# Tail of a two-stage image kernel: last tile normalised and split in three column pieces, output sum made by accumulating transposes

## The chip, the cores and the metric

The kernel runs on one core of a Trainium2 chip. The metric is the device time of one execution in microseconds (us), as the median of several runs. The core's engines run their own instruction streams and meet only at semaphores: TensorE (PE, with its weight loads shown apart as PEld), VectorE (DVE), ScalarE (ACT), GpSimd (POOL) and SyncE (SP), which here only issues DMAs.

## The reference, cut to what matters

The input `x` is (8, 32, 32, 64) float32. Two residual blocks follow each other:

```
x = x + diffusion(_gn(x), ...)     # 5 steps, then relu(bn(h))
x = x + conv(_gn(x), W, b)         # 3x3, 64 -> 64, ternary weights, relu(y + b)
return x
```

`_gn` subtracts the mean and divides by the standard deviation of each image and group of two channels. The second block is what the change touches: with x1 the output of the first block, it needs the statistics of x1, the normalised x1 (xn), the convolution of xn, `relu(alpha * conv + b)`, and at last x1 + that relu.

## The kernel before, in words

The eight images are two tiles of four (t = 0 and 1). The diffusion steps of the two tiles alternate in the order of the table `ORDER`; the last is step 4 of tile 1, so everything of the second block for tile 1 comes after all else. That tail is what the change is about.

Layout of the tail: a partition is one of a pair of image columns times a channel (2 x 64 = 128), the free dimension runs over 16 column pairs j, 32 rows h and 4 images b, so that one pair j takes 128 elements. Per tile:

- `residual` (DVE) adds x and the relu of block one into `coef[:, t, 2]` = x1 and takes its statistics; `spread` and `second_norm` (DVE with two small matmuls on PE and two tiny ACT operations) make scale and bias per image, and raise `norm_ready`.
- `normalise` writes xn into `odd_pairs(t)` = 17 shifted column pairs. The write crosses the two halves of the partitions: ACT does three operations of 64 x 512 and DVE five (its own four and the one for image 3), every one with a stride of four elements, since one operation takes one image. ACT counts `xn_ready`, DVE `xn_too`.
- `upper_half` (ACT) rounds xn to `hi`, `lower_half` (DVE) writes `lo` = xn - hi, in two pieces of columns each. For t = 1 the first piece has 5 of the 17 column pairs, the second 12.
- `dense(t, i)` (PE, line 1124) is the convolution: 12 matmuls of 512 columns per PSUM bank. Tile 0 has two parts of two banks (24 matmuls each), tile 1 has four parts of one bank (12 each), named `cf_t_i`.
- `relu_dense` (ACT) reads the PSUM of `cf_t_i` into `coef[:, t, 0]`. `output_sum` (DVE, line 851) adds x1 to it into `coef[:, t, 3]` and raises `sum_ready`. `out_natural(t, i)` (PE, line 957) transposes that back, 8 transposes for a part of tile 0 and 4 for one of tile 1, into `tb_t_i`; `take_out` (ACT) copies it to `coef[:, t, 4]`, and SP stores it (line 278).

PSUM has four slots. `job_table` gives each PE job its slot, and `take(name)` on PE waits until the reader of the job that held the slot before is done. `cf_0_1` and `cf_1_1` both have slot 3, `tb_0_0` and `cf_1_2` slot 0, `tb_0_1` and `cf_1_3` slot 1, `cf_0_0` and `cf_1_0` slot 2.

The order on each engine is written out by hand. In the tail it is:

```
ACT: normalise(1) upper_half(1) relu_dense(0,1) take_out(0,0) relu_dense(1,0) relu_dense(1,1) ...
DVE: normalise(1) output_sum(0,0) lower_half(1,0) lower_half(1,1) output_sum(0,1) output_sum(1,0..3)
PE:  dense(0,1) out_natural(0,0) dense(1,0) dense(1,1) out_natural(0,1) dense(1,2) out_natural(1,0)
     dense(1,3) out_natural(1,1) out_natural(1,2) out_natural(1,3)
```

All ACT operations go through one helper, so all have line 325.

Of the kernel before, what the change touches and what calls it, by code (L numbers as in the profile page):

```python
# [16 lines left out]
BT = B // TILES  # L17
# [61 lines left out]
def network(nc, x, wide_taps, norms, matrices, out_cols, conv_w, out):  # L79
# [11 lines left out]
    with ExitStack() as ctx:  # L91
# [3 lines left out]
        def sem(name):  # L95
            return ctx.enter_context(nc.semaphore(name))
# [71 lines left out]
        def part(ap, t, i):  # L168
            n = N // out_parts[t]
            return ap[:, i * n:(i + 1) * n]  # L170
# [5 lines left out]
        def odd_pairs(t):  # L176

            return coef[:, t, 3:5, :].rearrange("p a n -> p (a n)")[:, 0:(PAIRS + 1) * BT * H]

        def by_rows(ap, t, i):  # L180

            first = PAIRS // out_parts[t] + 1
            return ap.rearrange("p (j r) -> p j r", j=PAIRS + 1)[:, slice(0, first) if i == 0 else slice(first, None)]

        def slot_ap(name):
            return psum[:, slot_of[name], :]
# [28 lines left out]
            "wabs_ready", "kept_ready", "alpha_ready", "tern_ready"))  # L215
        mv_ready, q_ready, norm_ready, xn_ready, xh_ready, xl_ready = (sem(n) for n in (
            "mv_ready", "q_ready", "norm_ready", "xn_ready", "xh_ready", "xl_ready"))
        pads_ready, sum_ready = sem("pads_ready"), sem("sum_ready")

        edges_ready, xn_too = sem("edges_ready"), sem("xn_too")  # L220

        def wait_job(eng, name):

            eng.wait_ge(pe_job, job_no[name] + 1)

        def wait_reader(eng, name):

            eng.wait_ge(slot_free[slot_of[name]], uses_before[name] + 1)
# [86 lines left out]
        def _(act):  # L315
# [8 lines left out]
            def copy(dst, src, func=ACT.Copy, **kw):  # L324
                return nc.scalar.activation(dst, src, func, **kw)  # L325
# [144 lines left out]
                frees(copy(half(coef[:, t, 0, :], h), slot_ap(name), ACT.Relu, scale=outw[:, 2:3],  # L470
                           bias=outw[:, 3:4]), name)

            def normalise(t):

                act.wait_ge(norm_ready, t + 1)
                x1 = coef[:, t, 2, :].rearrange("p (j h b) -> p j h b", b=BT, h=H)
                to = odd_pairs(t).rearrange("p (j h b) -> p j h b", b=BT, h=H)
                for b in range(BT - 1):
                    copy(to[0:64, 1:, :, b], x1[64:128, :, :, b], ACT.Identity, scale=gn2[64:128, t, 3, b:b + 1],
                         bias=gn2[64:128, t, 4, b:b + 1]).then_inc(xn_ready, 1)  # L480

            def upper_half(t):

                act.wait_ge(pads_ready, 4)
                act.wait_ge(edges_ready, 2 * (t + 1))
                act.wait_ge(xn_ready, (BT - 1) * (t + 1))
                act.wait_ge(xn_too, (BT + 1) * (t + 1))
                for h in range(2):
                    if t:
                        wait_job(act, f"cf_0_{h}")  # L490
                    copy(by_rows(hi[:, :], t, h)[:, :, BT:BT + 128], by_rows(odd_pairs(t), t, h)).then_inc(xh_ready, 1)

            def relu_dense(t, h):

# [36 lines left out]
                wait_reader(act, f"nat_{k}_{t}_1")  # L531
                wrap(t, k + 1, halo_ready)
            rsqrt_first(128, BT)
            normalise(0)
            upper_half(0)
            relu_bn_out(1, 0)
            relu_bn_out(1, 1)
            relu_dense(0, 0)
            rsqrt_first(128, BT)
            normalise(1)  # L540
            upper_half(1)
            relu_dense(0, 1)
            take_out(0, 0)
            relu_dense(1, 0)
# [9 lines left out]
        def _(dve):  # L554
# [261 lines left out]
            def spread(t):  # L816

                wait_job(dve, f"mean2_{t}")
                frees(V.tensor_copy(gn2[:, t, 0, :], slot_ap(f"mean2_{t}")[:, 0:BT]), f"mean2_{t}")
                wait_reader(dve, f"mean2_{t}")  # L820
                then(V.tensor_tensor(gn2[:, t, 1, :], mv[:, t, :, 0], gn2[:, t, 0, :], ALU.subtract))
                then(V.tensor_tensor(gn2[:, t, 1, :], gn2[:, t, 1, :], gn2[:, t, 1, :], ALU.mult))
                signal(V.tensor_tensor(gn2[:, t, 2, :], mv[:, t, :, 1], gn2[:, t, 1, :], ALU.add), q_ready, t + 1)

            def second_norm(t):

                wait_job(dve, f"var2_{t}")
                rsqrt(128, BT, gn2[:, t, 3, :],
                      V.tensor_scalar(rs_in[:, 0:BT], slot_ap(f"var2_{t}")[:, 0:BT], GN2_EPS, None, ALU.add))
                leave(f"var2_{t}")  # L830
                signal(stt(gn2[:, t, 4, :], gn2[:, t, 0, :], -1.0, gn2[:, t, 3, :], ALU.mult, ALU.mult),
                       norm_ready, t + 1)

            def normalise(t):

                x1 = coef[:, t, 2, :].rearrange("p (j h b) -> p j h b", b=BT, h=H)
                to = odd_pairs(t).rearrange("p (j h b) -> p j h b", b=BT, h=H)
                for k, b in [(0, b) for b in range(BT)] + [(1, BT - 1)]:
                    p = slice(64 * k, 64 * k + 64)
                    V.tensor_scalar(to[64 * (1 - k):64 * (1 - k) + 64, k:k + PAIRS, :, b], x1[p, :, :, b],  # L840
                                    gn2[p, t, 3, b:b + 1], gn2[p, t, 4, b:b + 1], ALU.mult, ALU.add)\
                        .then_inc(xn_too, 1)

            def lower_half(t, h):
                dve.wait_ge(xh_ready, 2 * t + h + 1)
                V.tensor_tensor(by_rows(lo[:, :], t, h)[:, :, BT:BT + 128], by_rows(odd_pairs(t), t, h),  # L846
                                by_rows(hi[:, :], t, h)[:, :, BT:BT + 128].bitcast(f32), ALU.subtract).then_inc(xl_ready, 1)

            def output_sum(t, h):
                wait_reader(dve, f"cf_{t}_{h}")  # L850
                V.tensor_tensor(part(coef[:, t, 3, :], t, h), part(coef[:, t, 0, :], t, h),  # L851
                                part(coef[:, t, 2, :], t, h), ALU.add).then_inc(sum_ready, 1)

            def step(k, t, then_do=()):

                def then(i):
                    for at, what in then_do:
                        if at == i:
                            what()

                if k > 1 and not kept(k, t):
                    multiply(t, k + 1, A0, 0, 0)
                then(-1)
                if k == 0:
                    dve.wait_ge(s_halo, 4 * (t + 1))
                else:
                    dve.wait_ge(halo_ready, 4 * states_through(k - 1, t))
                for i, (a, dw, dc) in enumerate(((AYM, 0, -1), (AYP, 0, 1), (AXM, -1, 0), (AXP, 1, 0), (AE, 0, 0))):
                    multiply(t, k, a, dw, dc)
                    then(i)  # L870
                if k and k + 1 < STEPS and kept(k + 1, t):
                    dve.wait_ge(kept_free[t], k)
                    V.tensor_tensor(wc(first_two[t][:, :]), wc(coef[:, t, A0, :]), h_at(t, k), ALU.mult)\  # L873
                        .then_inc(kept_made[t], 1)
# [48 lines left out]
            for k, t in ORDER[2:-1]:  # L923
                step(k, t)
            residual(0)
            step(STEPS - 1, 1, ((-1, lambda: spread(0)), (1, lambda: second_norm(0)), (3, lambda: normalise(0))))
            lower_half(0, 0)
            lower_half(0, 1)
            residual(1)
            spread(1)  # L930
            second_norm(1)
            normalise(1)
            output_sum(0, 0)
            lower_half(1, 0)
            lower_half(1, 1)
            output_sum(0, 1)
            for q in range(4):
                output_sum(1, q)

        @blk.tensor  # L940
        def _(pe):
# [168 lines left out]
            def dense(t, i, first=0, last=None):  # L1110


                banks = 4 // out_parts[t]
                pe.wait_ge(xl_ready, 2 * t + 1 + (i > 0))
                dst = take(f"cf_{t}_{i}") if first == 0 else slot_ap(f"cf_{t}_{i}")
                for bank in range(banks):
                    j0 = 4 * (banks * i + bank)
                    to = dst[:, bank * BANK:(bank + 1) * BANK].rearrange("p (j r) -> p j r", r=128)
                    steps = [(b, dy, half_of) for b in range(2) for dy in range(3) for half_of in (hi, lo)]
                    for n, (b, dy, half_of) in enumerate(steps):  # L1120
                        if not first <= bank * len(steps) + n < (last or 1000):
                            continue
                        rows = half_of[:, :].rearrange("p (j r) -> p j r", j=PAIRS + 1)
                        ins = mm(to, dense_m[:, b, dy, :], rows[:, j0 + b:j0 + b + 4, dy * BT:dy * BT + 128],  # L1124
                                 start=(n == 0), stop=(n == len(steps) - 1))
                if last is None:
                    ins.then_inc(pe_job, 1)

            def out_natural(t, i):
                pe.wait_ge(sum_ready, out_parts[0] * t + i + 1)  # L1130
                src = part(coef[:, t, 3, :], t, i)
                turns(f"tb_{t}_{i}", [src[:, j * 128:j * 128 + 128] for j in range(16 // out_parts[t])])

            pe.wait_ge(mats_in, 16)
            def group_mean(t):
# [139 lines left out]
```

## Time and profile before

| | us |
|---|---|
| median of 3 runs | 340.66 (340.45, 340.66, 341.94) |
| the profiled execution, its own time | 342.05 |
| its span | 340.2 |
| PE busy / DVE busy / ACT busy | 258.7 / 270.1 / 137.3 |
| mean granted TensorE clock | 0.93 of full speed |

The span is the part of the execution that the trace covers; 342.05 - 340.2 = 1.85 us lie around it. A granted clock of 1.00 is 2.4 GHz and 0.50 is 1.2 GHz; TensorE has these two levels.

### The profile page before, as it was taken

Reading aid. Unit: us, or ns where it says so; the run is one execution under the profiler, and the core shown is the slowest. Engines: PE = TensorE matmul, PEld = TensorE weight load, DVE = VectorE, ACT = ScalarE, POOL = GpSimd, SP = SyncE. Lnnn points to the kernel's source line nnn. Section 1 sums busy time; section 2 is a strip of 40 time slices with the busy share of each in tenths; the row PEclk is TensorE's granted clock in tenths of the full one; section 3 lists DMA queues with packets and bytes.
Section 4 is the critical chain, followed back from the end, with each engine's and each line's share of the span. In section 5 each row is a group of like instructions: output and inputs, shape, how many; then the busy total and the mean of one; then the engine's idle time right before and its main releaser. Section 6 shows DMA issues by size and latency. Waiting matters only on the chain. (4 is left out here: it accounts for less than half of the span.)

```text
span 340.2 us, 4036 instructions
## 1 busy us (share of the span) xinstructions
PE 258.7 (76%) x1676; PEld 228.2 (67%) x1676; DVE 270.1 (79%) x224; ACT 137.3 (40%) x198; POOL 7.3 (2%) x25
## 2 busy tenths in 40 slices
PE   0116799929829799999502999999999987768794
PEld 0115688828728689668402999998989977656683
DVE  1895268848992575949999999999999999997811
ACT  3256579986002616260200332441522241452843
POOL 1000000000000000000100000110110000000000
PEclk9999899987958799999955899999999999999899
DMA  7596000000000000000230000633754003000033
GB/s 257 145 420 283 0 2 1 1 0 2 0 0 0 2 0 0 2 0 2 44 79 0 0 2 2 123 64 62 178 115 82 3 0 125 0 0 0 2 123 123
DMA packets 5169, 19.09 MB, mean 56 GB/s; under 512 B 2336, under 2 KB 2336, under 8 KB 3616
## 3 DMA queue, kind: packets, MB, share of 16 engines
q1 hardware_dynamic: 4144, 12.88, 10.6%
q0 software_dynamic: 720, 5.24, 7.6%
q10 hardware_dynamic: 288, 0.72, 0.7%
q8 instruction: 13, 0.21, 0.3%
q14 instruction: 4, 0.03, 0.0%
HBM read 11.50 MB, written 2.10 MB: 40 GB/s over the span
## 5 line engine op out<-in xcount | busy, mean ns | idle before, releaser
L797 DVE TENSOR_TENSOR ring<-coef,state 128x2048 f32<-128x2048 f32 x51 | 113.5, 2288 | 11.7 <-PE psum L1051 6.4
L1051 PE MATMUL psum<-mats,ring 128*128 128x128 f32 x816 | 94.5, 274 | 8.5 <-DVE ring L797 8.1
L1051 PEld LDWEIGHTS psum<-mats,ring 128*128 128x128 f32 x816 | 89.1, 141 | 12.3 <-DVE ring L797 12.0
L325 ACT ACTIVATE state<-psum 128x1024 f32<-128x1024 f32 x36 | 35.2, 1024 | 96.1 <-PE psum L1051 59.4
L1011 PE MATMUL psum<-coef,state 128*128 128x256 f32 x192 | 45.7, 390 | 0.0
L1011 PEld LDWEIGHTS psum<-coef,state 128*128 128x128 f32 x192 | 37.7, 196 | 5.4
L577 DVE SCALAR_TENSOR_TENSOR coef<-coef 128x2048 f32<-128x2048 f32 x15 | 34.4, 2291 | 3.4 <-ACT coef L325 3.1
L325 ACT ACTIVATE coef<-psum 128x512 f32<-128x512 f32 (+1 forms) x22 | 17.1, 789 | 39.7 <-PE psum L986 29.7
L1051 PE MATMUL psum<-mats,first_two 128*128 128x128 f32 x144 | 19.0, 290 | 18.6 <-DVE first_two L577 18.6
L986 PE MATMUL psum<-hi_s,sobel_m 128*128 128x512 f32 (+2 forms) x48 | 21.2, 446 | 13.2 <-DVE wred L581 7.4
L1051 PEld LDWEIGHTS psum<-mats,first_two 128*128 128x128 f32 x144 | 17.5, 151 | 19.1 <-issue 19.0
L986 PEld LDWEIGHTS psum<-hi_s,sobel_m 128*128 128x128 f32 x48 | 11.3, 236 | 16.1 <-issue 14.1
L1124 PE MATMUL psum<-hi,dense_m 128*128 128x512 f32 x48 | 20.4, 424 | 0.5 <-DVE lo L846 0.5
L1124 PE MATMUL psum<-lo,dense_m 128*128 128x512 f32 x48 | 19.8, 413 | 0.0
L986 PE MATMUL psum<-lo_s,sobel_m 128*128 128x512 f32 (+2 forms) x48 | 19.6, 430 | 0.0
L325 ACT ACTIVATE coef<-coef 128x2048 f32<-128x2048 f32 (+1 forms) x8 | 13.8, 1754 | 9.6 <-DVE coef L717 9.5
L325 ACT ACTIVATE coef<-coef,scales 128x384 f32<-128x384 f32 x32 | 16.7, 603 | 0.6 <-DMA coef<-in_wide_taps 0.6
L957 PE MATMUL psum<-mats,state 128*128 128x128 f32 x128 | 16.1, 282 | 0.3 <-ACT state L325 0.3
L957 PEld LDWEIGHTS psum<-mats,state 128*128 128x128 f32 x128 | 15.1, 147 | 0.6 <-ACT state L325 0.5
L325 ACT ACTIVATE ring<-state 128x2048 f32<-128x2048 f32 x4 | 11.4, 2854 | 5.9 <-DVE state L619 5.9
L851 DVE TENSOR_TENSOR coef<-coef 128x512 f32<-128x512 f32 (+1 forms) x6 | 5.2, 870 | 9.9 <-ACT coef L325 9.9
L986 PEld LDWEIGHTS psum<-lo_s,sobel_m 128*128 128x128 f32 x48 | 11.3, 235 | 2.0
(123 smaller groups left out, 273.9 us busy)
## 6 DMA issues: line engine op xcount, KB each, us to landing
coef<-in_wide_taps SPq DMA_DIRECT2D x4, 1536.0 KB, 11.5
first_two<-coef POOLq DMA_DIRECT2D x5, 1024.0 KB, 7.0
coef<-in_x SPq DMA_DIRECT2D x2, 1024.0 KB, 5.9
ring<-in_x SPq DMA_DIRECT2D x2, 512.0 KB, 7.0
ring<-in_x SPq DMA_DIRECT2D x1, 1024.0 KB, 9.6
out<-coef SPq DMA_DIRECT2D x2, 512.0 KB, 3.1
out<-coef SPq DMA_DIRECT2D x4, 256.0 KB, 3.0
mats<-in_matrices ACTq DMA_DIRECT2D x1, 384.0 KB, 6.6
```

What stands on the lines that cost most here:

```text
L325: return nc.scalar.activation(dst, src, func, **kw)
L577: return V.scalar_tensor_tensor(out=out_ap, in0=in0, scalar=scalar, in1=in1, op0=op0, op1=op1)
L797: V.tensor_tensor(wc(ring[:, slot, :]), wc(coef[:, t, a, :]), h_at(t, k, dw, dc), ALU.mult)\
L851: V.tensor_tensor(part(coef[:, t, 3, :], t, h), part(coef[:, t, 0, :], t, h), part(coef[:, t, 2, :], t, h), ALU.add).then_inc(sum_ready, 1)
L957: ins = nc.tensor.transpose(dst[:, j * 128:j * 128 + 128], src, ident)
L986: ins = mm(dst[:, bank * BANK + to * C:bank * BANK + (to + count) * C], sobel_m[:, m, :], part[:, frm * C:(frm + count) * C], start=(i == ...
L1011: ins = mm(to, sT[t][:, cg, dy * BT:dy * BT + 128], taps_m[:, cg, dy, :, :].rearrange("p v n -> p (v n)"), start=False, stop=(dy == 2), sk ...
L1051: ins = mm(slot_ap(name)[:, (j % 8) * 128:(j % 8) * 128 + 128], src[:, j * 128:j * 128 + 128], ident, is_transpose=True, start=first and j ...
L1124: ins = mm(to, dense_m[:, b, dy, :], rows[:, j0 + b:j0 + b + 4, dy * BT:dy * BT + 128], start=(n == 0), stop=(n == len(steps) - 1))
```

## The change

For tile 1 `normalise` on both engines takes a range of columns, and three pieces of columns (0 to 5, 5 to 9, 9 to 17) are normalised, rounded and split one after the other. Tile 0 keeps its two pieces and is normalised at once. `output_sum` is gone from DVE: `out_natural` now transposes x1 first and then the relu of the convolution into the same PSUM columns, accumulating, and so makes the sum on PE. The orders of ACT and PE are else as before; on DVE the pieces of `normalise` and `lower_part` alternate.

```
+        column_parts = (((0, 9), (9, 17)), ((0, 5), (5, 9), (9, 17)))
         def by_rows(ap, t, i):
-            first = PAIRS // out_parts[t] + 1
-            return ap.rearrange("p (j r) -> p j r", j=PAIRS + 1)[:, slice(0, first) if i == 0 else slice(first, None)]
+            return ap.rearrange("p (j r) -> p j r", j=PAIRS + 1)[:, slice(*column_parts[t][i])]
 ...
 # ACT
+            def normalise(t, columns):
+                j0, j1 = max(columns[0] - 1, 0), columns[1] - 1
 ...
+                    copy(to[0:64, j0 + 1:j1 + 1, :, b], x1[64:128, j0:j1, :, b], ACT.Identity,
+                         scale=gn2[64:128, t, 3, b:b + 1], bias=gn2[64:128, t, 4, b:b + 1]).then_inc(xn_ready, 1)
+            def upper_parts(t):
                 act.wait_ge(pads_ready, 4)
                 act.wait_ge(edges_ready, 2 * (t + 1))
-                act.wait_ge(xn_ready, (BT - 1) * (t + 1))
-                act.wait_ge(xn_too, (BT + 1) * (t + 1))
-                for h in range(2):
+                act.wait_ge(norm_ready, t + 1)
+                if t == 0:
+                    normalise(0, (0, PAIRS + 1))
+                    act.wait_ge(xn_ready, BT - 1)
+                    act.wait_ge(xn_too, BT + 1)
+                for i, columns in enumerate(column_parts[t]):
                     if t:
-                        wait_job(act, f"cf_0_{h}")
-                    copy(by_rows(hi[:, :], t, h)[:, :, BT:BT + 128], by_rows(odd_pairs(t), t, h)).then_inc(xh_ready, 1)
+                        normalise(1, columns)
+                        act.wait_ge(xn_ready, (BT - 1) * (i + 2))
+                        act.wait_ge(xn_too, (BT + 1) * (i + 2))
+                        wait_job(act, f"cf_0_{min(i, 1)}")
+                    copy(by_rows(hi[:, :], t, i)[:, :, BT:BT + 128], by_rows(odd_pairs(t), t, i)).then_inc(xh_ready, 1)
 ...
 # DVE
-            normalise(1)
-            output_sum(0, 0)
-            lower_half(1, 0)
-            lower_half(1, 1)
-            output_sum(0, 1)
-            for q in range(4):
-                output_sum(1, q)
+            normalise(1, column_parts[1][0])
+            normalise(1, column_parts[1][1])
+            lower_part(1, 0)
+            normalise(1, column_parts[1][2])
+            lower_part(1, 1)
+            lower_part(1, 2)
 ...
 # PE
-                pe.wait_ge(xl_ready, 2 * t + 1 + (i > 0))
+                pe.wait_ge(xl_ready, 2 * t + min(i + 1, len(column_parts[t])))
             def out_natural(t, i):
-                pe.wait_ge(sum_ready, out_parts[0] * t + i + 1)
-                src = part(coef[:, t, 3, :], t, i)
-                turns(f"tb_{t}_{i}", [src[:, j * 128:j * 128 + 128] for j in range(16 // out_parts[t])])
+                name, count = f"tb_{t}_{i}", 16 // out_parts[t]
+                dst = take(name)
+                for piece, ready in ((2, False), (0, True)):
+                    if ready:
+                        wait_reader(pe, f"cf_{t}_{i}")
+                    src = part(coef[:, t, piece, :], t, i)
+                    for j in range(count):
+                        ins = mm(dst[:, j * 128:j * 128 + 128], src[:, j * 128:j * 128 + 128], ident, is_transpose=True,
+                                 start=not ready and j % 4 == 0, stop=ready, skip_group_check=True)
+                ins.then_inc(pe_job, 1)
```

## Rows read from the trace of the kernel before

**Rows 1.** The chain of waits, tail: start us, us, what.

```profile
314.10 2.68 DVE coef L840 x4
316.81 0.74 DVE coef L840
317.58 1.24 DVE coef L851
318.87 1.09 PE psum L957 x8
319.96 7.13 PE psum L1124 x24
327.09 0.87 PE psum L957 x8
...
330.76 0.44 PE psum L957 x4
331.19 2.79 PE psum L1124 x12
...
334.07 0.79 ACT coef L325
...
334.88 0.70 DVE coef L851
...
335.63 0.67 PE psum L957 x4
...
336.32 0.60 ACT coef L325
```

**Rows 2.** Timeline of PE: start us, us, engine, line, operation [idle before <-releaser].

```profile
300.96 1.97 PE L1051 MATMUL psum<-mats,ring 128*128 128x128 f32 x16 [2.18 <-DVE ring L797]
...
316.58 0.39 PE L1124 MATMUL psum<-lo,dense_m 128*128 128x512 f32 x1
318.87 1.09 PE L957 MATMUL psum<-mats,coef 128*128 128x128 f32 x8 [1.90 <-DVE coef L851]
```

**Rows 3.** Stretches: busy us (count) of PE, PEld, DVE, ACT, POOL, granted clock, DMA.

```profile
299.00:301.00 2.00, 0.04 (x1) 0.04 (x1) 2.00 (x2) 1.81 (x2) 0.00 (x0) 1.00 0.00 0
301.00:303.00 2.00, 1.93 (x16) 1.69 (x16) 2.00 (x2) 0.91 (x1) 0.01 (x1) 1.00 0.00 0
322.00:323.00 1.00, 1.00 (x4) 0.81 (x3) 0.95 (x1) 0.02 (x1) 0.00 (x0) 0.50 0.00 0
```

**Rows 4.** Timeline of ACT and of DVE around the split of tile 1.

```profile
309.32 1.20 ACT L325 ACTIVATE coef<-psum,outp,wred 128x1024 f32<-128x1024 f32 x1 [4.93 <-PE psum L1124]
...
314.10 3.65 ACT L325 ACTIVATE coef<-coef,gn 64x512 f32<-64x512 f32 x3 [1.10 <-DVE gn L577]
317.91 2.12 ACT L325 ACTIVATE hi<-coef 128x640 fp32r<-128x640 f32 x2 [0.16 <-ACT coef L325]
319.92 1.19 ACT L325 ACTIVATE coef<-psum,outp,wred 128x1024 f32<-128x1024 f32 x1
```

**Rows 5.** Groups by shape: busy us, mean ns of one, idle before.

```profile
L325 ACT ACTIVATE coef<-coef,gn 64x512 f32<-64x512 f32 x6 | 7.4, 1310 | 2.2 <-DVE gn L577 2.2
L325 ACT ACTIVATE coef<-psum,outp,wred 128x512 f32<-128x512 f32 x4 | 3.1, 778 | 8.2 <-PE psum L1124 8.2
L325 ACT ACTIVATE hi<-coef 128x1024 fp32r<-128x1024 f32 x1 | 1.0, 1042 | 0.0
L325 ACT ACTIVATE hi<-coef 128x640 fp32r<-128x640 f32 x1 | 0.7, 738 | 0.2 <-ACT coef L325 0.2
L840 DVE TENSOR_SCALAR coef<-coef,gn 64x512 f32<-64x512 f32 x10 | 6.9, 747 | 0.1
L846 DVE TENSOR_TENSOR lo<-coef,hi 128x640 fp32r<-128x640 f32 x1 | 0.8, 819 | 0.0
```

**Rows 6.** Stretches in which PE makes only transposes (columns of rows 3).

```profile
188.00:190.00 2.00, 2.00 (x12) 2.00 (x11) 2.00 (x2) 0.00 (x0) 0.00 (x0) 0.50 0.00 0
206.00:208.00 2.00, 2.00 (x21) 2.00 (x20) 2.00 (x2) 0.00 (x0) 0.00 (x0) 1.00 0.00 0
```

More of the change, by code:

```diff
@@ L217, in network @@
             "mv_ready", "q_ready", "norm_ready", "xn_ready", "xh_ready", "xl_ready"))
-        pads_ready, sum_ready = sem("pads_ready"), sem("sum_ready")
+        pads_ready = sem("pads_ready")
         edges_ready, xn_too = sem("edges_ready"), sem("xn_too")
@@ L471, in relu_bn_out @@
                            bias=outw[:, 3:4]), name)
-            def normalise(t):
-                act.wait_ge(norm_ready, t + 1)
+            def normalise(t, columns):
+                j0, j1 = max(columns[0] - 1, 0), columns[1] - 1
                 x1 = coef[:, t, 2, :].rearrange("p (j h b) -> p j h b", b=BT, h=H)
@@ L478, in normalise @@
                 for b in range(BT - 1):
-                    copy(to[0:64, 1:, :, b], x1[64:128, :, :, b], ACT.Identity, scale=gn2[64:128, t, 3, b:b + 1],
-                         bias=gn2[64:128, t, 4, b:b + 1]).then_inc(xn_ready, 1)
-            def upper_half(t):
+                    copy(to[0:64, j0 + 1:j1 + 1, :, b], x1[64:128, j0:j1, :, b], ACT.Identity,
+                         scale=gn2[64:128, t, 3, b:b + 1], bias=gn2[64:128, t, 4, b:b + 1]).then_inc(xn_ready, 1)
+            def upper_parts(t):
                 act.wait_ge(pads_ready, 4)
                 act.wait_ge(edges_ready, 2 * (t + 1))
-                act.wait_ge(xn_ready, (BT - 1) * (t + 1))
-                act.wait_ge(xn_too, (BT + 1) * (t + 1))
-                for h in range(2):
-                    if t:
-                        wait_job(act, f"cf_0_{h}")
-                    copy(by_rows(hi[:, :], t, h)[:, :, BT:BT + 128], by_rows(odd_pairs(t), t, h)).then_inc(xh_ready, 1)
+                act.wait_ge(norm_ready, t + 1)
[4 more added lines that the diff above has]
+                for i, columns in enumerate(column_parts[t]):
+                    if t:
+                        normalise(1, columns)
[3 more added lines that the diff above has]
+                    copy(by_rows(hi[:, :], t, i)[:, :, BT:BT + 128], by_rows(odd_pairs(t), t, i)).then_inc(xh_ready, 1)
             def relu_dense(t, h):
@@ L533, in _ @@
             rsqrt_first(128, BT)
-            normalise(0)
-            upper_half(0)
+            upper_parts(0)
             relu_bn_out(1, 0)
@@ L539, in _ @@
             rsqrt_first(128, BT)
-            normalise(1)
-            upper_half(1)
+            upper_parts(1)
             relu_dense(0, 1)
@@ L832, in second_norm, with normalise @@
                        norm_ready, t + 1)
-            def normalise(t):
+            def normalise(t, columns):
+                first, end = columns
                 x1 = coef[:, t, 2, :].rearrange("p (j h b) -> p j h b", b=BT, h=H)
@@ L838, in normalise, with lower_part @@
                 for k, b in [(0, b) for b in range(BT)] + [(1, BT - 1)]:
+                    j0, j1 = max(first - k, 0), min(end - k, PAIRS)
                     p = slice(64 * k, 64 * k + 64)
[L840 to L852, printed above, removed]
+                    V.tensor_scalar(to[64 * (1 - k):64 * (1 - k) + 64, j0 + k:j1 + k, :, b], x1[p, j0:j1, :, b],
+                                    gn2[p, t, 3, b:b + 1], gn2[p, t, 4, b:b + 1], ALU.mult, ALU.add).then_inc(xn_too, 1)
+            def lower_part(t, i):
+                dve.wait_ge(xh_ready, 2 * t + i + 1)
+                V.tensor_tensor(by_rows(lo[:, :], t, i)[:, :, BT:BT + 128], by_rows(odd_pairs(t), t, i),
+                                by_rows(hi[:, :], t, i)[:, :, BT:BT + 128].bitcast(f32), ALU.subtract).then_inc(xl_ready, 1)
             def step(k, t, then_do=()):
@@ L925, in _ @@
             residual(0)
-            step(STEPS - 1, 1, ((-1, lambda: spread(0)), (1, lambda: second_norm(0)), (3, lambda: normalise(0))))
-            lower_half(0, 0)
-            lower_half(0, 1)
+            step(STEPS - 1, 1, ((-1, lambda: spread(0)), (1, lambda: second_norm(0)), (3, lambda: normalise(0, (0, PAIRS + 1)))))
+            lower_part(0, 0)
+            lower_part(0, 1)
             residual(1)
@@ L931, in _ @@
             second_norm(1)
-            normalise(1)
-            output_sum(0, 0)
-            lower_half(1, 0)
-            lower_half(1, 1)
-            output_sum(0, 1)
-            for q in range(4):
-                output_sum(1, q)
+            normalise(1, column_parts[1][0])
[4 more added lines that the diff above has]
+            lower_part(1, 2)
         @blk.tensor
```

## The prediction

> **What bounds the kernel now.** I read the page first, then the chain of waits over the last 30 us, then the timelines of PE, ACT and DVE over that stretch, and last the granted clock in short stretches. The change touches nothing ahead of 314.10 us, where scale and bias of tile 1 are known, so only the last 26 us count. In the chain [rows 1] the reader is to see three pieces. From 314.10 to 318.87 it runs through DVE: five operations of normalise and then the output sum of tile 0's first part, line 851. From 318.87 to 334 it is PE alone and without a gap: transposes (line 957) and dense matmuls (line 1124). The end is one part's way out: relu on ACT, sum on DVE, four transposes, copy on ACT. So in this tail PE is the bound for 15 us, and whatever adds work to PE there is paid in full.
>
> Two losses lie beside it. PE stands idle for 1.90 us before 318.87, until line 851 is done [rows 2]. And soon after this idle time the granted clock is 0.50, that is 1.2 GHz [rows 3]: 24 dense matmuls take 7.13 us where 12 at full clock take 2.79 [rows 1], so 7.13 - 5.58 = 1.55 us are lost to the clock.
>
> **The sum moved to PE.** Each `out_natural` has twice the transposes: 32 more over the tail. Eight take 0.87 us and four take 0.44 [rows 1], 0.11 us each, so this adds 32 x 0.11 = 3.52 us to an engine that is the bound. Accumulating transposes are not new in the kernel: in the diffusion steps they run at 21 in 2.00 us, 0.10 each [rows 6], so the bounds are 3.2 and 3.5 us and I take 3.52, the rows with the same source. The six sums leave DVE. Five of them lay beside PE work and bring nothing. What their going brings is on PE, in two places:
> - Before 318.87: `out_natural(0,0)` no longer waits for normalise and the sum, only for the relu of `cf_0_0`, which ended at 310.52 [rows 4]. PE goes on right behind the last matmul of `dense(0,1)`, started at 316.58; one of 12 in 2.79 takes 0.23, so from 316.81. Gain 318.87 - 316.81 = 2.06 us. With this gap the cause of the slow clock goes too: 1.55 us more, if no other gap takes its place (below).
> - At the end: the last dense matmul leaves PE at about 331.19 + 2.79 less the tail of one, 333.81. Then PE made 8 transposes (0.88) and stood until 335.63: 0.94 us. Now 24 transposes follow without a wait, since the relu of `cf_1_3` (0.79 [rows 1]) is done long before the third part's turn. Gain 0.94 us; the 12 extra transposes are in the 3.52.
>
> **Three pieces.** Per piece ACT makes 3 operations of 4, 4 and 8 column pairs, 128, 128 and 256 elements, in place of 3 of 512; DVE makes 5 each. No such small strided operation is in the trace. The cost of one at 512 is 1.31 us on ACT [rows 5]. Its fixed part: the relu with scale and bias from columns takes 1.20 us at 1024 [rows 4] and 0.778 at 512 [rows 5], so 0.36 at zero; I take 0.38, and the slope is (1.31 - 0.38)/512. Then 128 elements cost 0.61, 256 cost 0.85. Three of 512 took 3.65 us and not 3.93 [rows 4], so neighbours overlap by 0.14. A group of three is 3 x 0.61 - 0.28 = 1.55 us, of 256 it is 3 x 0.85 - 0.28 = 2.27. Each group ends in a wait of ACT for its own last write, 0.16 [rows 4], and the rounding copy of the piece: 0.74 for 640 elements, 1.04 for 1024 [rows 5], 0.63 for 512 between. The sum of `upper_parts(1)` is 1.55 + 1.55 + 2.27 + 3 x 0.16 + 0.74 + 0.63 + 1.04 = 8.26, less 3 overlaps, 7.84 us, against 319.92 - 314.10 = 5.82 before [rows 4]. So the relu of `cf_0_1`, next in ACT's queue, starts at 321.94 and ends 1.20 later, at 323.14, 2.0 us later than before. From below: if cost goes by elements alone, only the added copy (0.2) and two waits (0.3) remain, 0.5 us later. From above: nine operations each as dear as one of 512 would make it 5 us later still than I say. My value is nearest to the rows because every other ACT form has two sizes and falls with size.
>
> The Trainium skill (ScalarE: Activation LUTs, What ACT_TABLE_LOAD costs) gives an activation 186 ns, 93 more for each column operand, and 0.833 ns an element. Its fixed part, 0.37 us, agrees with my 0.38; its 0.80 us for 512 elements does not agree with the 1.31 of this strided form [rows 5]. By its figures for the small ones an estimate is 0.48 and 0.59 us, which would bring the relu forward by some 1.4 us; the trace decides here.
>
> DVE: 512 elements cost 0.747 [rows 5], five of them 2.68 + 0.74 = 3.42 in all [rows 1]; with 0.2 fixed, five of 160 or 128 are some 1.6 and 1.5 us. First piece done 315.7, second 317.2, then `lower_part(1,0)` 0.82 [rows 5]: 318.0. PE wants it at 318.57. It is covered by 0.5 us; without that cover it would cost one for one.
>
> **The new wait.** PE's `dense(1,1)` takes slot 3, which `cf_0_1` holds until its relu has read it. Before, that read ended at 321.1 and PE came there later, so it cost nothing. Now PE comes early: 316.81 + 16 transposes (1.76) = 318.57, + `dense(1,0)` 2.79 = 321.36. The slot comes free at 323.14 + 0.05. PE stands for 1.84 us. Behind it on PE stands everything: `out_natural(0,1)`, two dense parts and the last transposes. The slots of the later jobs are free in time: `take_out(0,0)` ends at some 324.2 and `dense(1,2)` wants slot 0 at 327.8.
>
> **The sum.** + 3.52 (transposes) + 1.84 (new wait) - 2.06 (old gap) - 0.94 (gap at the end) - 1.55 (slow clock) = + 0.81 us against the profiled execution. The same by the clock: 323.2, + 2.79 + 1.76 + 2.79 + 0.88 + 2.79 = 334.2, + 24 x 0.11 = 336.85, + 0.23 for the last one to finish (0.67 against 0.44 for four [rows 1]), + 0.62 copy = 337.7 against 336.92. Span 341.0, own time 342.85.
>
> How that stands to the runs: the profiled execution took 342.05, the median 340.66, one run 341.94. The difference of 1.4 is about the 1.55 of the slow clock, so I take it that the two quicker runs didn't have that stretch. Against those, the same sum without the clock's term is + 2.36, from 340.66 to 343.0. If the 1.4 belonged to profiling alone, it would be 341.5. I forecast 342.9.
>
> **Rivals.**
> - *The clock falls after the new wait.* For it: the old gap of 1.90 us was followed by 1.2 GHz [rows 2, 3], and mine is 1.84. Against it: a gap of 2.18 us before 300.96 [rows 2] left the clock at 1.00, from 299 to 303 [rows 3]. So gaps of this size go either way. The fall costs 1.55 us again: 344.4.
> - *Not slower: ACT's small operations are cheap.* Place: the three groups in `upper_parts(1)`. If their cost goes by elements, the relu of `cf_0_1` ends at 321.6 and the wait is 0.3 in place of 1.84 us: 342.85 - 1.5 = 341.3, and at the clock state of the median 341.5. It decides from a 128-element operation under some 0.45 us. Against it: the 0.38 of fixed cost in the other ACT forms.
> - *Faster.* ACT cheap, and the runs of before mostly with the slow stretch, the runs of after without: + 0.81 - 1.5 = -0.7 from 340.66, 340.0; below 339 nothing in the rows leads.
> - *Transposes don't hold the clock.* If PE's clock dropped in the longer runs of transposes, the 24 at the end would take 0.17 each (12 in 2.00 us at 0.50 [rows 6]) and not 0.11: + 1.4 us, 344.3. Against it: 21 transposes in 2.00 us stand in a stretch that holds transposes alone, with the clock at 1.00 [rows 6]. The Trainium skill (TensorE: Matmul & The Clock Gate, Part 4: PE-mode transpose) says that transposes don't count as busy in the way of matmuls; the trace of this kernel does not agree.
>
> **Chances.** Forecast as it stands (wait of 1.5 to 2.2 us, clock at full) 0.45; clock falls after the wait 0.22; transposes lose the clock 0.03; cheap ACT operations or the profiling offset 0.26; faster 0.04. A difference of 0.5%, 1.7 us, is what a measurement of this kernel can tell from none: slower means above 342.4, faster below 339.0. The forecast lies 0.5 us above the first bound, so a part of its 0.45, some 0.1, counts as no change. That gives slower 0.60, same 0.36, faster 0.04. The range runs from the cheap case with its median clock to the case of the fallen clock, 341.2 to 344.6.
>
> **What would show it.** In the changed trace: `out_natural(0,0)` right behind the last matmul of `dense(0,1)`, at about 316.8; no slow clock at 320 to 323; ACT's 64x128 operations at 0.61 us and its relu of `cf_0_1` at about 322; PE idle some 1.8 us before `dense(1,1)` with ACT as releaser; line 1124 at 2.79 per 12; 24 transposes at the end with no gap, and the last copy of ACT ending near 337.7. It is wrong if the relu of `cf_0_1` ends before 321.5, or if `lower_part(1,0)` comes after 318.6 and PE waits for DVE before `dense(1,0)`.

## The result and the profile after

| | before | after |
|---|---|---|
| median of 20 runs | 341.1 us | 342.6 us |
| lowest to highest | 339.98 to 342.22 | 341.69 to 345.14 |
| the profiled execution | 342.05 | 341.9 |
| its span | 340.2 | 340.1 |

The ratio after to before is 1.005, with a 95% interval of 1.0031 to 1.0069: the changed kernel is half a per cent slower. Four of its 20 runs stand apart at 344.8 to 345.1. The two profiled executions show almost the same span, so the spans alone would mislead. What differs is where the tail begins. DVE's first normalise operation of tile 1 starts at 314.10 us before [rows 1] and at 312.73 after, for a reason ahead of all that the change touches (last section). From there to the end of the last copy on ACT is 22.82 us before (336.32 + 0.60 - 314.10) and 24.14 after (336.27 + 0.60 - 312.73): + 1.32 us. I call this the tail, and compare tails below.

The chain of waits after, of the tail: start us, us, what. It answers to [rows 1].

```profile
310.87 4.73 PE psum L1124 x20
315.60 1.75 PE psum L1138 x16
317.35 2.97 PE psum L1124 x12
320.32 0.02 issue
320.34 0.02 ACTq L225
320.36 0.72 issue
321.07 1.20 ACT coef L326
322.27 0.14 issue
322.41 3.02 PE psum L1124 x12
325.42 1.75 PE psum L1138 x16
327.17 2.79 PE psum L1124 x12
329.96 0.87 PE psum L1138 x8
330.83 2.78 PE psum L1124 x12
333.62 2.63 PE psum L1138 x24
336.25 0.02 issue
336.27 0.60 ACT coef L326
```

DVE is gone from it: but for one relu and the last copy, both on ACT, all is PE, dense matmuls (L1124) and accumulating transposes (L1138). The break at 320.32 to 322.41 is the new wait. The timelines of PE and of ACT show both sides of it:

```profile
319.92 0.39 PE L1124 MATMUL psum<-lo,dense_m 128*128 128x512 f32 x1
322.41 0.47 PE L1124 MATMUL psum<-hi,dense_m 128*128 128x512 f32 x1 [2.10 <-ACT coef L326]
```

```profile
312.81 1.61 ACT L326 ACTIVATE coef<-coef,gn 64x128 f32<-64x128 f32 x3 [1.18 <-DVE gn L582]
314.65 0.74 ACT L326 ACTIVATE hi<-coef 128x640 fp32r<-128x640 f32 x1 [0.24 <-ACT coef L326]
315.42 1.65 ACT L326 ACTIVATE coef<-coef,gn 64x128 f32<-64x128 f32 x3
317.11 0.63 ACT L326 ACTIVATE hi<-coef 128x512 fp32r<-128x512 f32 x1
317.76 2.32 ACT L326 ACTIVATE coef<-coef,gn 64x256 f32<-64x256 f32 x3
320.11 1.06 ACT L326 ACTIVATE hi<-coef 128x1024 fp32r<-128x1024 f32 x1
321.07 1.19 ACT L326 ACTIVATE coef<-psum,outp,wred 128x1024 f32<-128x1024 f32 x1
```

ACT works from 312.81 with no pause but one of 0.24 us, yet comes to the relu of `cf_0_1` only at 321.07, 8.26 us after it began; before it took 5.82 [rows 4]. PE has been ready since 320.3. The small operations cost, by the groups by shape (busy us, mean ns):

```profile
L326 ACT ACTIVATE coef<-coef,gn 64x128 f32<-64x128 f32 x6 | 3.3, 611 | 1.2 <-DVE gn L582 1.2
L326 ACT ACTIVATE coef<-coef,gn 64x256 f32<-64x256 f32 x3 | 2.3, 841 | 0.0
L847 DVE TENSOR_SCALAR coef<-coef,gn 64x128 f32<-64x128 f32 x6 | 2.1, 396 | 0.1
```

The granted clock (the figure after POOL's) around the wait, to set beside [rows 3]:

```profile
302.00:304.00 2.00, 2.00 (x7) 1.59 (x6) 1.97 (x3) 1.20 (x1) 0.40 (x2) 0.50 0.00 0
318.00:320.00 2.00, 2.00 (x10) 1.53 (x9) 1.94 (x5) 2.00 (x3) 0.00 (x0) 1.00 0.00 0
320.00:322.00 2.00, 0.31 (x2) 0.00 (x0) 0.97 (x2) 1.97 (x3) 0.00 (x0) 1.00 0.00 0
322.00:324.00 2.00, 1.59 (x7) 1.36 (x8) 0.43 (x1) 1.85 (x3) 0.00 (x0) 1.00 0.00 0
```

The slow clock behind the old gap is gone, and none follows the new wait in this execution. At 302 to 304 PE is slow in `dense(0,0)`, but DVE sets the pace there: it is still at the statistics of tile 1, for which PE waits afterwards.

### The profile page after: what moved, and what is told of

Same layout as the page of the kernel before. It is cut to its first block and busy times, and to the rows that moved or that the text cites. A ratio compares the mean times of both kernels' runs of the same rounds, so it can differ in the third digit from the quotient of the medians.

```text
span 340.1 us, 4108 instructions
## 1 busy us (share of the span) xinstructions
PE 260.9 (77%) x1708; PEld 230.9 (68%) x1708; DVE 267.5 (79%) x229; ACT 139.8 (41%) x205; POOL 7.2 (2%) x25
## 5 line engine op out<-in xcount | busy, mean ns | idle before, releaser
L1051 PE MATMUL psum<-mats,ring 128*128 128x128 f32 x816 | 95.5, 275 | 8.8 <-DVE ring L802 8.6
L986 PE MATMUL psum<-hi_s,sobel_m 128*128 128x512 f32 (+2 forms) x48 | 19.7, 414 | 13.0 <-DVE wred L586 7.2
L1124 PE MATMUL psum<-hi,dense_m 128*128 128x512 f32 x48 | 20.1, 419 | 2.1 <-ACT coef L326 2.1
L986 PEld LDWEIGHTS psum<-hi_s,sobel_m 128*128 128x128 f32 x48 | 10.4, 216 | 15.6 <-issue 13.8
L1124 PE MATMUL psum<-lo,dense_m 128*128 128x512 f32 x48 | 19.3, 403 | 0.0
L986 PE MATMUL psum<-lo_s,sobel_m 128*128 128x512 f32 (+2 forms) x48 | 18.3, 404 | 0.0
L1124 PEld LDWEIGHTS psum<-hi,dense_m 128*128 128x128 f32 x48 | 9.4, 196 | 4.7 <-issue 2.7
L986 PEld LDWEIGHTS psum<-lo_s,sobel_m 128*128 128x128 f32 x48 | 10.4, 216 | 1.8
```

The costliest lines, as they stand in the source:

```text
L986: ins = mm(dst[:, bank * BANK + to * C:bank * BANK + (to + count) * C], sobel_m[:, m, :], part[:, frm * C:(frm + count) * C], start=(i == ...
L1051: ins = mm(slot_ap(name)[:, (j % 8) * 128:(j % 8) * 128 + 128], src[:, j * 128:j * 128 + 128], ident, is_transpose=True, start=first and j ...
```

## The experiments

All ratios are to the kernel before on the same chip. Theory: the new wait for slot 3 and the added transposes cost more than the two gaps and the slow clock give back. Rivals: the wait only shows slack; the transposes hide; the slow clock has another cause; the pieces carry the change.

**e1, relu taken up early.**

```
 # ACT, upper_parts(t), at the end of the loop over the pieces
+                    if t and i == 1:
+                        relu_dense(0, 1)
 ...
             upper_parts(1)
-            relu_dense(0, 1)
```

> The changed kernel with one edit: on ScalarE the relu of the part cf_0_1 is taken up right after the second rounding copy, ahead of the third piece's normalise. Theory (the slot-3 wait of PE is a price of the change): the 2.1 us wait before dense(1,1) is gone, the third piece's lower part comes 1.2 us later and is still hidden; 2.1 us less than the changed kernel, so about 340.5 us, 0.6 below the kernel before. Rival (the wait is only where the slack of the longer PE work shows, another input of dense(1,1) or dense(1,2) is late next): less than 0.7 us gained, 342 us.

Measured: 341.14 us, ratio 0.9983 (0.9967 to 0.9998). Against the 1.005 of the changed kernel this is 0.67%, 2.3 us, less. The chain of waits has no break any more, and the tail is 22.01 us (313.12 to 335.13), 2.13 less than after:

```profile
316.01 1.75 PE psum L1139 x16
317.75 5.92 PE psum L1125 x24
323.68 1.75 PE psum L1139 x16
```

The wait is a full loss and little takes its place: the 24 matmuls took 5.92 us where e5 (below) has 5.56, partly because the weight loads of `dense(1,0)` and `dense(1,1)` waited for DVE's lower parts, 0.5 us in all. Moving one line takes the changed kernel from slower than before to a little faster.

**e2 and e10, mixed: transposes where PE would stand, VectorE sums elsewhere.**

```
 # on top of e1, with output_sum defined on DVE as in the kernel before; PE
+                order = [(0, 1), (1, 0), (1, 1), (1, 2)]
+                if (t, i) in order:
+                    pe.wait_ge(sum_ready, order.index((t, i)) + 1)
+                    src = part(coef[:, t, 3, :], t, i)
+                    turns(name, [src[:, j * 128:j * 128 + 128] for j in range(count)])
+                    return
 # DVE
             lower_part(1, 1)
+            output_sum(0, 1)
             lower_part(1, 2)
+            for q in range(3):
+                output_sum(1, q)
 # job_table: tb_1_3 in slot 2, not 1
```

> The changed kernel with the early relu, and accumulating transposes only where PE would stand otherwise (tile 0's first part, tile 1's last part, which goes to PSUM slot 2 so that x1 can be laid down ahead of its relu); the other four sums are made on VectorE as before. Theory (each of the 32 added transposes costs PE 0.11 us wherever PE is the bound): 20 fewer transposes save 2.2 us, the last part waits only for its relu and four transposes; with the wait gone 4.4 us less than the changed kernel, 338.2 us, 2.9 below the kernel before. Rival (the sums on VectorE come late and give the waits back): 340 us or more.

> The mixed kernel once more, as the yardstick on the same chip. Theory: 2.3 us faster than the kernel before. Rival (the first measurement was a lucky one): 1 us faster.

Measured: e2 339.54 us, ratio 0.9933 (0.9909 to 0.9957); e10 339.22 us, 0.9946 (0.9930 to 0.9962). This beats both kernels, the one before by some 0.6% and the changed one by some 1.1%, but by less than expected: by the ratios 2.3 us (e2) and 1.8 us (e10) against the kernel before, for 2.9 and 2.3. The tail of e10 is 19.83 us (313.78 to 333.61), 4.31 less than after, where 4.4 was expected. Its chain of waits:

```profile
316.66 1.75 PE psum L1153 x16
318.41 5.95 PE psum L1133 x24
324.36 0.87 PE psum L966 x8
325.23 2.79 PE psum L1133 x12
328.02 0.44 PE psum L966 x4
328.46 2.79 PE psum L1133 x12
...
331.33 2.28 ACT coef L326 x4
```

Where L966 stands, the sum came from DVE and PE pays half as many transposes (8 and 4, where after has 16 and 8). At the end ACT's relu and its three copies follow each other without a wait. The medians moved less than the tails (e10's tail is 2.99 us shorter than that of the kernel before). Why is open in the main; e2's own trace shows one reason, a slow stretch in `dense(0,1)` behind PE's wait for the mean (20 matmuls in 6.31 us, where others have 4.73), which made its tail 21.02.

**e3, transposes only.** The edit is the change's `out_natural` in the kernel before, with all `output_sum` calls removed.

> The kernel before with the sum made by accumulating transposes, tile 1 still normalised at once and split in two pieces. Theory: 24 later transposes add 2.64 us, the gap at the end gives 0.94 back, the first gap shrinks from 1.9 to about 0.9 us (now for lower_half(1,0)) and the slot-3 wait does not appear; 1.5 us slower than the kernel before at equal clock, 0.7 to 1.5 over all runs, 342.0 to 342.6. Rival (transposes hide beside the waits): within 0.3 us of the kernel before.

Measured: 341.56 us, ratio 0.9997 (0.9982 to 1.0012). The expected 0.7 to 1.5 us slower did not come. The tail is 22.79 us (313.07 to 335.86), as before. The transposes didn't hide: PE's chain has them all. PE still stood before `dense(1,0)`, for 0.91 us, and the clock stayed at 1.00.

```profile
318.60 5.82 PE psum L1120 x24
324.41 1.75 PE psum L1134 x16
326.16 2.79 PE psum L1120 x12
328.95 0.87 PE psum L1134 x8
329.82 2.78 PE psum L1120 x12
332.60 2.63 PE psum L1134 x24
```

What balances them, beside the shorter gap and the sums that are gone at the end, is the clock: 24 matmuls in 5.82 us, in 7.13 before [rows 1]. I had weighed the slow clock as present in part of the executions; e5 shows how much it is worth.

**e4, pieces only.**

```
 # the changed kernel; PE's out_natural and DVE's output_sum as before, and on DVE
             normalise(1, column_parts[1][1])
+            output_sum(0, 0)
             lower_part(1, 0)
             normalise(1, column_parts[1][2])
             lower_part(1, 1)
+            output_sum(0, 1)
             lower_part(1, 2)
+            for q in range(4):
+                output_sum(1, q)
```

> The changed kernel with the sums back on VectorE (the first one ahead of lower_part(1,0), as before), so only the three pieces of columns are left of the change. Theory: ScalarE's nine small operations make the relu of cf_0_1 2.1 us later, the gap of 1.9 us on PE before out_natural(0,0) stays, and the slot-3 wait is about 0.8 us: 0.8 us slower than the kernel before, 341.9. Rival (finer pieces start dense(1,0) earlier and pay for themselves): 0 to 1 us faster than before.

Measured: 342.14 us, ratio 1.0012 (0.9994 to 1.0030); not told apart from no change. The tail is 23.09 us (314.27 to 337.36), + 0.27. The slot-3 wait of 0.8 is not there:

```profile
317.92 1.24 DVE coef L857
319.16 0.04 issue
319.20 1.09 PE psum L966 x8
320.30 7.23 PE psum L1133 x24
```

The 24 matmuls again run partly at 1.2 GHz and take 7.23 us, so PE comes later to `dense(1,1)`. The relu is in time, though barely: it ends at 324.37 and `dense(1,1)` starts at 324.51. The slow clock covered the wait; I had added the two.

**e5, the gap before `dense(1,0)` filled.**

```
 # the kernel before; PE, ahead of the wait of out_natural(0, 0)
+                    fill = take("tb_0_0")
+                    x1 = part(coef[:, 0, 2, :], 0, 0)
+                    for j in range(16):
+                        nc.tensor.transpose(fill[:, (j % 8) * 128:(j % 8) * 128 + 128],
+                                            x1[:, (j % 8) * 128:(j % 8) * 128 + 128], ident)
```

> The kernel before with 16 transposes whose result nobody uses (x1 into the free slot of tb_0_0) on PE ahead of the wait for the first output sum; they fit the gap of 1.9 us, the sum and all else stay. Theory (the 1.2 GHz stretch after that gap comes from the gap and costs 1.55 us in most executions): 1.5 us less than the kernel before, its slow stretch at 320 to 323 gone; if only every second execution has it, 0.8 us less. Rival (the slow stretch has another cause, or other executions don't have it): within 0.3 us of the kernel before.

Measured: 339.59 us, ratio 0.9945 (0.9926 to 0.9965). Sixteen transposes of no use make the kernel before 1.9 us faster. The tail is 21.28 us, 1.54 less:

```profile
317.57 1.09 PE psum L957 x8
318.66 5.56 PE psum L1124 x24
```

So the gap causes the slow stretch. The gain over all runs is 1.2 to 2.5 us by the interval, which leaves no room for a stretch that only every second execution has, and five of the six runs are below 340.16, the quickest of the 20 of the kernel before on this chip. So most executions of the kernel before have it, the quick ones too; that all have it is not shown. The experiment also rejects that transposes leave the clock low.

**e11, the kernel before, a second trace.**

> The kernel before, for a second trace. Theory (its gap of 1.9 us on PE brings the slow clock in every execution, whatever the early part did): a stretch of 1.2 GHz in tile 1's dense matmuls again, and 22.8 us from the first normalise operation to the end of the last copy. Rival (the slow stretch is in some executions only): no such stretch and 21.3 us.

One run, 342.01 us, and again a slow stretch, with a tail of 22.81 us.

```profile
318.00:320.00 2.00, 1.18 (x10) 1.13 (x10) 1.50 (x2) 2.00 (x3) 0.00 (x0) 1.00 0.00 0
320.00:322.00 2.00, 2.00 (x7) 1.53 (x6) 2.00 (x2) 1.98 (x2) 0.00 (x0) 0.54 0.00 0
322.00:324.00 2.00, 2.00 (x7) 1.64 (x6) 0.90 (x1) 0.00 (x0) 0.00 (x0) 0.61 0.38 154
```

**e6, the new wait filled, and e8, the changed kernel again.** e6 puts the same 16 transposes, of tile 0's second part, into slot 1 ahead of `dense(1,1)` in the changed kernel.

> The changed kernel with 16 unused transposes (1.75 us) in the 2.10 us wait before dense(1,1). Nothing gets shorter by them. Theory (the fifth of its executions near 345 us are those in which the clock falls after that wait): no execution above 344 us, the rest as the changed kernel, median 342.3 to 342.6. Rival (the executions near 345 come from another place): some of them stay near 345.

> The changed kernel once more, as the yardstick on the same chip for the filled one and for a second trace. Theory: 1.5 us slower than the kernel before, one execution in five near 345 us; where the trace has a stretch of 1.2 GHz after PE's wait before dense(1,1), its tail is 1.55 us longer than in the first trace. Rival (the early part of the kernel makes the difference between executions): tail of the same length, 24.1 us from the scales to the last copy, in any execution.

Measured: e6 342.89 us, ratio 1.0043 (1.0029 to 1.0057), its 12 runs between 341.52 and 343.38; e8 342.90 us, 1.0041 (1.0021 to 1.0060), eight of its nine runs up to 343.45 and one at 345.00. The tails are 24.17 and 24.15 us. e8 confirms the size of the change. No run near 345 in 12 with the wait filled, against 5 in 29 without, fits a clock that falls after the new wait, but is too few to show it: at 5 in 29, twelve runs without one have a chance of about one in ten. The five have a mean granted clock of 0.925, the lowest of the 29 (0.925 to 0.940), which points to the clock; where in the kernel, no trace shows, for none caught such an execution.

**e7, mixed with two pieces.** The edit of e2 on the kernel before, without the three pieces and the early relu.

> The kernel before (tile 1 normalised at once, two pieces, relu of cf_0_1 after both) with accumulating transposes only for tile 0's first part and tile 1's last part, the last in slot 2, as in the mixed kernel. Theory: the three pieces are worth only the earlier start of dense(1,0), 0.9 us; 0.9 us slower than the mixed kernel, 1.4 us faster than the kernel before. Rival (the pieces are what makes the mixed kernel fast): no faster than the kernel before.

Measured: 339.66 us, ratio 0.9947 (0.9931 to 0.9964). The tail is 20.57 us, 0.74 more than e10's. By the ratios e7 can't be told from e2 and e10. The pieces bring about 0.7 us in the tail, and only where the relu doesn't wait behind them.

**e9, mixed, with the wait for the mean filled.**

```
             dense(0, 0)
+            fill = take("cf_0_1")
+            for j in range(8):
+                nc.tensor.transpose(fill[:, j * 128:j * 128 + 128], ones[:, :], ident)
             group_mean2(1)
```

> The mixed kernel with 8 unused transposes (0.9 us) on PE between dense(0,0) and the small matmul of tile 1's mean, where PE stands 0.4 to 1.3 us and after which the clock fell in the mixed kernel's trace (dense(0,1) 1.55 us longer). Theory: that fall goes, 0.5 to 1 us less than the mixed kernel over all executions, 338.3 to 338.8 us. Rival (the filler is late where the gap is only 0.4 us and delays the mean by as much as it wins): within 0.3 us of the mixed kernel.

Measured: 338.82 us, ratio 0.9934 (0.9916 to 0.9953), against 0.9946 of e10: the intervals overlap, so a gain of 0.4 us is possible and not shown. The tails are the same, 19.84 and 19.83, and can't decide it: neither of the two traces has the slow stretch of e2 in `dense(0,1)`.

## Why the prediction was right

342.9 was forecast, as slower, and 342.6 measured. Point by point:

- *The transposes, + 3.52.* Right. Eight take 0.87 us and 24 take 2.63 in the chain after, 0.11 each, with the clock at 1.00 throughout; e10 took 20 of them away from e1's kernel and the tail fell by 2.18 us, what they cost (2.2).
- *The gap before 318.87, - 2.06.* Right: `out_natural(0,0)` follows the last matmul of `dense(0,1)` at once (315.60 in the chain).
- *The gap at the end, - 0.94.* Right: 24 transposes without a wait, and the relu was in time.
- *The slow clock, - 1.55.* Right in size and cause; e5 gives 1.54 in the tail.
- *The new wait, + 1.84.* Right in place and mechanism, somewhat mis-sized: 2.10 by the trace. The single operations were right (611 and 841 ns for 0.61 and 0.85 us; the copy of 512 elements 633 ns for 0.63). What I undercounted lies between them: I took off 0.14 us for each change from a copy to the next group, where the timeline shows none (314.65 + 0.74 = 315.39, next start 315.42), the first wait for ACT's own write was 0.24 and not 0.16, and after the relu it took 0.14 us, not 0.05, until PE went on. Together `upper_parts(1)` took 8.26 us for a forecast 7.84.
- *The sum, + 0.81.* The tail measures + 1.32. The slot came free 9.68 us after the start of the tail (322.41 - 312.73), where 9.10 was forecast: 0.58 later. Only 0.26 of this shows as a longer wait, since PE itself came there 0.33 later than forecast (next point, and the last matmul ahead of a wait counts with its whole 0.39 us and not with 0.23). Behind the wait `dense(1,1)` took 3.02 us for a forecast 2.79, and the end took some 0.3 less than forecast.
- *`lower_part(1,0)` covered by 0.5 us.* This was wrong, and cost nothing here. DVE's small operations cost more than I took (396 ns at 128): the ten of the first two pieces lasted 3.62 us for a forecast 3.1, and `lower_part(1,0)` was done at 317.21. The cover was gone, and the weight load of `dense(1,0)` waited for it, which the chain of waits doesn't show:

```profile
317.26 0.19 PEld L1124 LDWEIGHTS psum<-hi,dense_m 128*128 128x128 f32 x1 [0.15 <-DVE lo L852]
```

  That is the wait for DVE that I had named as a sign of being wrong. Here the longer wait for slot 3 swallows it; in e1, without that wait, it is paid.
- *How it stands to the runs.* This step was wrong, and the forecast is as near as it is partly by luck. I took the 1.4 us between the profiled execution and the median as the slow stretch, absent in the quicker runs. e5 shows that the quick ones have it too. At least a part of the spread arises far earlier (last section). With the tail's + 0.81 alone the forecast for the runs would have been 341.5 to 341.9; the tail's real + 1.32 on the 341.1 of 20 runs gives 342.4, which is the median of the 16 runs that don't stand near 345; with those four it is 342.6.
- *Rivals.* Cheap ACT operations: rejected by the 611 ns. (Two slips that bear on no sum: operations of 0.48 and 0.59 us, weighed in the prediction, would have brought the relu forward by 1.6 us and not 1.4, and nine operations at 1.31 us would have put it 5.6 us later and not 5.) Transposes that lose the clock: rejected by e5 and by the trace after. A fall of the clock after the new wait: in neither of the two traces of the changed kernel; the runs near 345 leave it open, and they lie 2.6 us above the median of the others and not 1.55.

## What to carry to other kernels

Before an operation is cut into pieces on an engine, look at what is queued behind the last piece on that engine and who holds a buffer until it runs: here nine small ACT operations pushed back one relu, the relu held a PSUM slot, and the bottleneck engine stood 2.10 us; one moved call gave it back. Work moved onto the engine that bounds the stretch is worth it only at the places where that engine would stand anyway (two of six sums here), so mix rather than convert. And a gap on PE costs more than its length if the clock falls behind it: here 1.9 us of waiting cost 1.55 us more, as much as a useless filler won back.

## What the runs showed that I had not expected

The start of the tail moves between executions without any change ahead of it. In seven traces (after, e1, e3, e5, e6, e7, e8) the first normalise operation starts at 312.30 to 313.12 us; in the others (before, e2, e4, e9, e10, e11) at 313.56 to 314.27. The seven have 1.2 GHz on PE at about 300 to 304 us, but that is not the reason: e10 has it too, from 302 on, and the difference is much older. The same group of transposes of the diffusion steps starts at 162.52 before and at 161.11 after, and in all thirteen traces the tail starts 151.6 to 151.7 us behind that group. Between before and after the lag is 0.55 us at 99.8 us and 1.3 at 114.4; what makes it there is open. The runs of the kernel before, 30 on one chip, lie in two groups, 340.3 to 341.1 and 341.4 to 342.3; that these are the two kinds of start is not shown, as both traces of the kernel before (342.05 and 342.01) are of the later kind. For a change of half a per cent it means that two profiled executions can be compared from a common instruction onward, and not by their spans: the spans here, 340.2 and 340.1, had hidden all of the loss.

A gap on PE of a given length does not decide by itself whether the clock falls: 1.9 us at 317 did in both traces of the kernel before, 2.10 us at 320 did not in both of the changed one, and 0.91 us did not in e3. The wait of 2.18 us before the transposes at 300.96 [rows 2] stands, with 2.18 to 2.20 us, in twelve of the thirteen traces, with nothing changed ahead of it. Less than 2 us after its end PE is at 1.2 GHz in eight of them, and not in the other four, the first trace of the kernel before among them [rows 3].
